# Filler products on TensorE in the opening's waits, split one-column offsets, and a new order of the opening on VectorE, ScalarE, POOL and SyncE

## What is computed

```python
xn = _layernorm(x, axis=-1)
x = x + attention_block(xn) + ffn(xn)
```

## Time and profile before

| what | us |
|---|---|
| median of 3 runs | 1043.35 (1042.75 to 1045.15) |
| the profiled execution | 1043.39 |
| its span | 1041.6 |
| PE busy in the span | 1002.9 |
| VectorE busy | 749.3 |
| ScalarE busy | 602.8 |
| POOL busy | 239.7 |

### The profile page before, as it was taken

How to read it: one execution, slowest core, us unless ns; L and a number is a source line. 1 busy time by engine, 2 the same in 40 slices (tenths; PEclk the granted TensorE clock), 3 DMA queues, 4 the chain that set the end, 5 groups by cost and what they waited for, 6 DMA issues and landing times.

```text
span 1041.6 us, 17189 instructions
## 1 busy us (share of the span) xinstructions
PE 1002.9 (96%) x6628; PEld 899.2 (86%) x6628; DVE 749.3 (72%) x965; ACT 602.8 (58%) x875; POOL 239.7 (23%) x221
## 2 busy tenths in 40 slices
PE   3999999999999999999999999999999999999998
PEld 3778887888877787788899989989999999999998
DVE  6874689534547768888876486876878978777765
ACT  4788667667435374565655545555647554665444
POOL 3444255233504000000000131331301322112210
PEclk9999999999999999999999999999999999999999
DMA  8989715956685744533402673225493423222310
GB/s 309 417 248 364 245 52 187 343 205 197 241 317 197 240 127 160 182 102 141 142 22 81 247 278 102 94 90 182 172 381 124 134 82 122 92 76 85 114 42 22
DMA packets 68803, 181.20 MB, mean 174 GB/s; under 512 B 5057, under 2 KB 26177, under 8 KB 65089
## 3 DMA queue, kind: packets, MB, share of 16 engines
q1 hardware_dynamic: 68720, 180.08, 49.9%
HBM read 122.39 MB, written 66.06 MB: 181 GB/s over the span
## 4 chain that ended last, share of the span: by engine, by line
PE 65%; DVE 8%; issue 5%; DMA 3%; ACT 3%; POOL 0%; SPq 0%; DVEq 0%; ACTq 0%
PE pr L2286 41%; PE pr L206 12%; PE pr L2482 8%; DMA h_s<-u 2%; DVE xp_lo L2014 1%; PE pr L2433 1%; PE pr L199 1%; DMA qa<-q_s 1%; PE pr L2264 1%; DVE x L1570 1%; PE pr L192 1%; DMA h_s<-silu 1%; ACT u L1444 1%; DVE u L2020 0%; ACT xp_hi L1428 0%
## 5 line engine op out<-in xcount | busy, mean ns | idle before, releaser
L2286 PE MATMUL pr<-xp_hi,wb 128*128 128x256 f32 x1344 | 315.5, 280 | 2.9 <-DVE u L2020 1.7
L2286 PE MATMUL pr<-xp_lo,wb 128*128 128x256 f32 x1344 | 314.7, 279 | 0.0
L2286 PEld LDWEIGHTS pr<-xp_hi,wb 128*128 128x128 f32 x1344 | 251.9, 187 | 5.2 <-issue 5.1
L2286 PEld LDWEIGHTS pr<-xp_lo,wb 128*128 128x128 f32 x1344 | 253.3, 188 | 0.0
L2286 PE MATMUL pr<-u_hi,ring 128*128 128x512 f32 x256 | 102.4, 400 | 1.8 <-POOL u_lo L948 1.0
L2286 PE MATMUL pr<-u_lo,ring 128*128 128x512 f32 x256 | 100.0, 391 | 0.0
L1428 ACT CAST xp_hi<-tf 128x1024 fp32r<-128x1024 f32 x48 | 50.2, 1047 | 57.2 <-PE pr L2286 19.9
L2014 DVE TENSOR_TENSOR xp_lo<-tf,xp_hi 128x1024 fp32r<-128x1024 f32 x48 | 61.9, 1290 | 19.5 <-ACT xp_hi L1428 19.4
L2482 PE MATMUL pr<-wf_hi,h_hi 128*128 128x256 f32 x256 | 74.6, 291 | 0.0
L2482 PE MATMUL pr<-wf_lo,h_hi 128*128 128x256 f32 x256 | 71.6, 280 | 0.0
L2482 PE MATMUL pr<-wf_hi,h_lo 128*128 128x256 f32 x256 | 71.5, 279 | 0.0
(11 more groups left out here) (236 smaller groups left out, 2508.7 us busy)
## 6 DMA issues: line engine op xcount, KB each, us to landing
ring<-w_s SPq DMA_DIRECT2D x42, 512.0 KB, 7.5
uf<-h_s SPq DMA_DIRECT2D x16, 1024.0 KB, 5.1
wb<-s_s SPq DMA_DIRECT2D x8, 1024.0 KB, 10.1
wb<-w_s SPq DMA_DIRECT2D x6, 1024.0 KB, 11.1
vw<-v_s SPq DMA_DIRECT2D x8, 514.0 KB, 7.5
xt<-x SPq DMA_DIRECT2D x8, 512.0 KB, 6.0
xn_s<-xh SPq DMA_DIRECT2D x8, 512.0 KB, 8.9
stage<-w_gated SPq DMA_DIRECT2D x2, 2048.0 KB, 12.9
```

Of the source, the lines that this page charges most:

```text
L2286: return e.matmul(bank, w.bitcast(dt), v_.bitcast(dt), start=first, stop=last, skip_group_check=True)
```

## The change

On PE, five products of 512 columns in F32 (acc with itself, results never read) are issued as soon as acc is cleared and before the wait for the parameters. `keep_running(count)` issues that many products of 128 columns (identity with itself) into the same unused bank; 8, 3, 3, 22 and 4 of them stand between the steps of the opening. The sixteen one-column records of the offsets are split into two halves, one ahead of a_channels(1) and one behind it. On VectorE, norm_moments(0) stands ahead of xn_moments(2), xn_moments(3) moves from the opening's middle to behind norm_moments(1), and the checks of pieces 4 and 5 move from ahead of norm_moments(1) to behind xn_moments(3); a wait for PE's first transposes, which come behind the fillers that read acc, stands ahead of the first check. On ScalarE, high_of_xg(0) moves ahead of copy_xn(1), and apply_xn(3) from behind copy_xn(2) to behind the first two ffn units of step -1. On POOL, low_of_xg(0) waits for the taps of tile 0, and inverse_deviation(3) moves behind that of the second norm of tile 1. On SyncE, stage group 1 is issued right behind group 0, and x(2) and x(3) follow groups 1 and 2 instead of groups 0 and 1.

```diff
--- before.py
+++ after.py
@@ -740,8 +740,8 @@
                 first, last = group[0], group[-1] + 1
                 sp.dma_start(stage_at[first // 4][:, first % 4:first % 4 + last - first, :],
                              w_gated[first:last].rearrange("n p c -> p n c")).then_inc(s["stage_in"][n], 16)
-                if n < 2:
-                    load_x(2 + n)
+                if n in (1, 2):
+                    load_x(1 + n)
                 if n == 1:
                     save_xn(0)
             save_xn(1)
@@ -969,12 +969,13 @@
             inverse_deviation(1, "a", "a_applied")
             halo(0, xh, "xh_w", 1, "xh_halo")
             halo(1, xh, "xh_w", 1, "xh_halo")
+            pool.wait_ge(s["b_taps"], 2)
             low_of_xg(0, xg1_lo, mid(xh[0]), xg1_hi)
             inverse_deviation(0, "b", "b_applied")
             inverse_deviation(2, "a", "a_applied")
-            inverse_deviation(3, "a", "a_applied")
             halo(2, xh, "xh_w", 1, "xh_halo")
             inverse_deviation(1, "b", "b_applied")
+            inverse_deviation(3, "a", "a_applied")
             halo(0, xi, "c_xi", KC, "xi_halo")
             for i in P1_STEPS:
                 front("p", i, "first")
@@ -1220,19 +1221,20 @@
 
             copy_xn(0)
             conv1_centre(0)
+            high_of_xg(0, xg1_hi, mid(xh[0]))
             copy_xn(1)
             split_attn_weights()
-            high_of_xg(0, xg1_hi, mid(xh[0]))
             conv1_centre(1)
             apply_norm(0)
             apply_xn(2)
             high_of_norm(0)
             copy_xn(2)
-            apply_xn(3)
             xi_out(0)
             act_out(0)
             for i in P1_STEPS:
                 front("p", i, "first")
+                if i < 0:
+                    apply_xn(3)
                 if valid(i + 1) and i >= 0:
                     xi_out(i + 1)
                 if i == 4:
@@ -1703,11 +1705,11 @@
             apply_xn(1)
             e.wait_ge(s["prm_in"], 32)
             conv1_side(0, False)
+            e.wait_ge(s["a_tr"], 1)
             check_staged(range(0, 1))
             conv1_side(0, True)
+            norm_moments(0)
             xn_moments(2)
-            norm_moments(0)
-            xn_moments(3)
             norm_offsets(0, "b", "b_applied")
             low_of_attn_weights()
             check_staged(range(1, 3))
@@ -1717,9 +1719,9 @@
             conv1_side(1, False)
             conv1_side(1, True)
             set_flag(0, front_bank[0][0:1, 0:1])
-            check_staged(range(4, 6))
             norm_moments(1)
-            check_staged(range(6, 7))
+            xn_moments(3)
+            check_staged(range(4, 7))
             for i in P1_STEPS:
                 front("p", i, "first")
                 if i < 0:
@@ -2175,7 +2177,15 @@
 
         @block.tensor
         def _(e):
+            e.wait_ge(s["checked"], 1)
+            for n in range(5):
+                e.matmul(front_bank[2], acc[:, 0:P].bitcast(F32), acc[:, 0:TOK].bitcast(F32), start=True, stop=True)
             e.wait_ge(s["prm_in"], 32)
+
+            def keep_running(count):
+
+                for n in range(count):
+                    e.matmul(front_bank[2][:, 0:P], ident[:], ident[:], start=True, stop=True)
 
             def attn_w(w, name, m):
                 at_ = A_COLS[name] + m * P
@@ -2184,13 +2194,14 @@
             def chunk(buf):
                 return lambda k: buf[:, k, :]
 
-            def offsets_of_weights():
+            def offsets_of_weights(*parts):
                 e.wait_ge(s["wf_in"], 16)
-                for j in range(2 * KC):
+                for j in parts:
                     for k in range(KC):
                         last = e.matmul(pr[2][:, 0, j:j + 1], wa_raw[:, k, j * P:(j + 1) * P], par("norm1_b", k),
                                         start=(k == 0), stop=(k == KC - 1))
-                last.then_inc(s["offsets"], 1)
+                if j == 2 * KC - 1:
+                    last.then_inc(s["offsets"], 1)
 
             def a_channels(i):
                 e.wait_ge(s["a_applied"], i + 1)
@@ -2323,10 +2334,16 @@
 
             def opening():
                 a_channels(0)
+                keep_running(8)
+                offsets_of_weights(0, 1)
                 a_channels(1)
-                offsets_of_weights()
+                keep_running(3)
+                offsets_of_weights(2, 3)
+                keep_running(3)
                 norm_tokens(0)
+                keep_running(22)
                 norm_back(0)
+                keep_running(4)
                 a_channels(2)
                 in_proj(0)
                 e.wait_ge(s["biased"], 1)
```

## The result

The changed kernel takes 1049.73 us, median of 7 runs (1046.71 to 1051.85). In the same session the kernel before took 1045.15 (7 runs, 1042.59 to 1045.89). The ratio is 1.0047, 95% interval [1.0032, 1.0061]: slower by 4.9 us of 1045, between 3.3 and 6.4. The direction was forecast; the time lies 1.8 us above the range. The forecast was added to a median of three runs (1043.35), and the session's median of the same kernel is 1.8 us above that. The profiled execution took 1051.85, span 1050.1; it is the longest of the seven.

The account below looks back on a forecast made before the run. PE is busy 96% of the span, but VectorE sets when the opening ends. The profiled 1043.39 plus 3.1 for the later hidden layer gives 1046.5, less 0.2 for collisions: 1046.3, range 1042.3 to 1047.9 us.

Parts of the forecast that it names:

- the three places named: VectorE idles before norm_moments(0) 1.2 us, before its checks after low_of_norm(0) 2.1, before norm_moments(1) 1.6.
- The pause itself: PE waits for VectorE before the third gate unit, from 40.5 to 45.1, a pause of 4.6 us.
- the sum: Whole kernel: +3.1 us from the later hidden layer, with 0.2 taken off for POOL's and VectorE's collisions.
- in_proj(0) 30.3, twelve products in 2.8 us: PE's first projection starts at 30.3 and runs at the higher clock level, putting PE 2.1 us ahead at the first layer.
- the predicted 66.8: Start of the hidden layer on PE after staged_bits(1) ends at 65.6; 3.1 us later than 63.70.
- POOL held once more and PE slow after the pause: Upper end of the likeliest case: a check holds each POOL operation again, units 2 and 3 run slow; +4.5 us.
- no row shows a fall from the higher level: Remark on PE's clock before the change; by the skill's rule the pause would still slow units 2 and 3, sum +3.5.
- PE's lead (faster): Rival 2: VectorE does not decide, PE's lead of 2.1 to 3.2 us stays; 1041.3 to 1040.2, chance 0.12.
- Nearly cancel: Rival 1: quick inverse_deviation(2) or lucky collisions, gated(0) at 43.1, +1.9 or less, within 0.2%; chance 0.33.
- The fillers don't raise the clock: Rival 3: fillers at the lower level push norm_back(0) from 26.57 to about 36; +9, 1052, chance 0.03.
- The load order at nothing: Moved loads in the opening cost nothing: x(2), wanted by VectorE at 21.0, stays hidden even with a 10 us landing.
- From 63.70 on PE is busy almost without a break, so this stays to the end: After the opening: the hidden layer's +3.1 us carries through to the kernel's end.

Follow-up runs that it names:

- e5: Changed kernel with more fillers: 12 instead of 4 behind norm_back(0), 4 behind a_channels(2), 16 in the pause before the third gate unit; 1047.27 us, ratio 1.0020.
- e3: Changed kernel with the checks of pieces 4 and 5 back ahead of norm_moments(1); 1045.78 us, ratio 1.0017 to the kernel before.
- e6: e4 with the old load order as well; 1044.08 us, ratio 0.9991 to the kernel before.
- e7: e6 with seven more fillers behind a_channels(2); 1041.09 us, ratio 0.9967 to the kernel before.
- e4: Changed kernel with tile 3's xn moments, inverse deviation and apply_xn, and the checks, in their old places; 1047.89 us, ratio 1.0029.
- e2: Changed kernel without fillers and with the offsets in one piece, new orders kept; 1051.17 us, ratio 1.0071.
- e1: Kernel before with only the fillers, the split offsets and the wait for a_tr, every order as before; 1044.42 us, ratio 1.0004.

## Why the prediction was right and wrong

**Right, and shown.** The fillers raise the clock and delay nobody (9.49, 18.09). VectorE loses time in the three places named: 1.19 us written 1.2, then 3.09 for 2.1 and 3.65 for 1.6 (1.78 in e5, with in_proj(0) at its quick pace). The three checks end up between norm_moments(1) and gated(0); e3 undoes that alone and PE's pause goes from 4.50 to 1.85. The pause itself is 4.50 us for 4.6, because it depends only on what stands between norm_tokens(1) and gated(0). silu(2) stands behind apply_xn(3) on ScalarE:

```profile
48.40 0.62 ACT L1198 CAST u_hi<-full 128x512 fp32r<-128x512 f32 x1 [4.56 <-DVE full L1690]
48.93 2.07 ACT L1067 ACTIVATE xt<-xt,nb_h,rs_a 128x256 f32<-128x256 f32 x4
50.91 0.66 ACT L1214 ACTIVATE silu<-pr,prm 128x512 f32<-128x512 f32 x1
51.48 0.60 ACT L1198 CAST u_hi<-full 128x512 fp32r<-128x512 f32 x1
51.99 1.92 ACT L1067 ACTIVATE xnt<-pr,nb_b,rs_b 128x256 f32<-128x256 f32 x4
```

apply_norm(1) starts 6.5 us later than in the earlier trace rows, written 3.3; the rest of it is gated(0)'s own lateness. In the changed kernel that chain does not decide, though: gated(2) and gated(3) wait for the slow PE (52.30, 54.66). With the clock held it does: gated(3) waits for ScalarE's silu in e5, 6.95 us behind gated(0), where the prediction had 7.0. With the clock held (e5) the whole loss is 2.1 us, [1.1, 3.0], where the sum had 2.9 to 3.1: the part of the order was sized at the upper end of what the runs allow.

**The step that failed** is "in_proj(0) 30.3, twelve products in 2.8 us". It priced those products at the higher level because the fillers had raised the clock, although its own timetable lets PE stand idle ahead of them (apply_xn(2) from 25.9 to 28.0). They ran at the lower level and took 5.4 us; in e5, with the clock held, they took 3.05. Against the predicted 66.8 the hidden layer came at 70.62, 3.8 later: 0.8 because POOL was held once more (in_proj(0) at 31.08 for 30.3), 2.6 in in_proj(0) itself, and the rest, 0.4, with the slow third gate unit, which leaves PE late for the units behind it. The range went up to "POOL held once more and PE slow after the pause", both of which came true, and had no term for this one.

The working did weigh a fall, for the pause alone, at +0.4 us. The Trainium skill, TensorE: Matmul & The Clock Gate, section "Why this matters for your kernels", tells to avoid gaps between bursts of matmuls; the rule was applied to one of the two gaps. The fall in the pause agrees with it (4.50 us, granted 0.77). The other came behind two shorter waits with transposes between, which no run here takes apart. And the sentence "no row shows a fall from the higher level" was true only because in the opening of before the clock had not yet risen when PE waited long.

**The rivals.** PE's lead (faster) is refuted with its condition: gated(0) came at 47.62, not near 39.9. It does come near in e6 (40.20) and e7 (40.51), and e7 is the only one faster. "Nearly cancel" is outside the interval. "The fillers don't raise the clock" is refuted by the first transposes.

**The load order at nothing** was wrong in its reason: x(2) was safe, x(3) was not, and it stayed hidden only because xn_moments(3) moved back too (e4, e6).

**Size and spread.** The profiled run lost 8.5 us, the medians differ by 4.6. It was the slowest of its seven (mean granted clock 0.992, the others 0.993 to 0.996), 2.2 us of it are the last store, and the profiled run of before was among its quicker ones. The forecast stood on one profiled execution and the median of three runs of a kernel whose runs differ by 3 us. It wrote 2.9 us above that median; set on the session's 1045.15 it would have been 1048.1, with the range up to 1049.7, and the measured 1049.73 lies 1.6 above. So about half of the 3.4 us by which the time was missed is the base, and the other half the loss itself. All seven runs have a mean granted clock of 0.992 to 0.996, against 0.998 to 1.000 in e5's eleven: the falls are no matter of the profiled run alone.

"From 63.70 on PE is busy almost without a break, so this stays to the end" holds only roughly. By the profiles, the shift at the hidden layer and at the last add is +6.9 and +6.2 in the changed kernel, +6.8 and +8.0 in e2, +4.3 and +2.2 in e5.

## What to carry to other kernels

Fillers that raise the clock gain most if they last until the real products begin (e5, e7), and nothing where another engine uses up the lead (e1): count each wait behind the last filler as a possible fall, and price the products behind it at both levels. An operation that waits for PE must not stand ahead of work that could fill that wait, above all on the engine that is the late one; put the independent checks first (e3). When a load is moved, follow every load behind it to its reader, not only the one that was moved.

## What was not expected of the hardware

- The clock fell not only in the pause of 4.50 us but also between 26.81 and 31.08, where PE waited 2.07 us, ran eight transposes and waited 0.65: granted 0.80, then 0.52. In e1 2.07 us, eight transposes and 1.12 us had the same effect on the products behind them.
- It does not do so alike in each run. e3 has the same work ahead of in_proj(0) as the changed kernel and rose two products in. An idle of 1.57 us brought a fall in e7, idles of 1.61 and 1.86 us brought none in e6. Twelve runs of e1 show how time goes with the clock, if not where it fell: the four with a mean granted clock of 0.995 took 1046.01 to 1047.75 us, the eight at 0.997 to 1.000 took 1041.98 to 1045.01.
- Before its first rise the clock column reads 1.00 while transposes take 1.94 us; in these traces the column shows falls, and the durations are what tells the level.
- The last store ends 3.3 to 3.6 us after the start of the last add in six of the twelve profiles and 5.2 to 5.6 in the other six, at the same code: 2 us of a single profile's time that no edit here explains. Its cause is open.
